# A gated cross-attention and mixture-of-experts block: queue orders of the attention written anew, scores of two pairs interleaved, one spread matmul a chunk

## The reference

```python
# attention of layernorm(x) to the context
q, k, v = proj(hs, Wq, bq), proj(at, Wk, bk), proj(at, Wv, bv)
scores = clip(einsum('bhsd,bhtd->bhst', q, k) / sqrt(32), -50, 50)
scores = clip(where(attend, scores, -10000.0), -50, 50)
probs = softmax(scores); probs = probs / (probs.sum(-1) + 1e-8)
delta = rs * ((probs @ v) @ Wo.T + bo)
x = x + tanh(g_xattn) * (layernorm(delta) * ln_gamma + ln_beta)
# experts on h = layernorm(x): 8 experts, the best 2 of each token
probs = softmax(h @ gate_weight.T); top_v, top_i = top_k(probs, 2)
y = sum_e w_e * (silu(gate_e) * up_e) @ down_e.T
x = x + tanh(g_ffn) * y
```

## Time and profile before

| | us |
|---|---|
| three runs | 991.68, 992.07, 988.66; median 991.68 |
| profiled execution | 987.01, of it span 984.8 |
| attention, to the last second layernorm | 0 to 264.6 |
| routing | 264.6 to 298.8 |
| expert loop | 298.8 to 984.8 |

### The profile page before, as it was taken

How to read it: one execution, slowest core, us unless ns; L and a number is a source line. 1 busy time by engine, 2 the same in 40 slices (tenths; PEclk the granted TensorE clock), 3 DMA queues, 4 the chain that set the end, 5 groups by cost and what they waited for, 6 DMA issues and landing times.

```text
span 984.8 us, 14350 instructions
## 1 busy us (share of the span) xinstructions
PE 910.5 (92%) x4217; PEld 714.1 (73%) x4218; DVE 450.3 (46%) x767; ACT 381.1 (39%) x717; POOL 257.3 (26%) x305
## 2 busy tenths in 40 slices
PE   4979999997819999999999999999999999999994
PEld 4746767664607888888888888888888888888883
DVE  5648778676586121261361352721452253217211
ACT  3555655643413222352452443522442253236221
POOL 4034627274231111122122122211131121122111
PEclk9999999997858999999999999999999999999997
DMA  7030121202636211171272262622352145121121
GB/s 305 13 117 0 71 102 48 79 37 93 240 114 269 43 21 32 33 276 33 42 267 37 60 245 43 240 61 40 105 204 32 21 134 186 21 42 22 21 43 21
DMA packets 27905, 93.92 MB, mean 95 GB/s; under 512 B 5424, under 2 KB 5424, under 8 KB 21104
## 3 DMA queue, kind: packets, MB, share of 16 engines
q1 hardware_dynamic: 18528, 72.03, 19.6%
q0 software_dynamic: 8640, 20.62, 11.0%
q10 hardware_dynamic: 720, 1.07, 0.3%
HBM read 75.03 MB, written 18.68 MB: 95 GB/s over the span
## 4 chain that ended last, share of the span: by engine, by line
PE 86%; DVE 4%; issue 3%; DMA 3%; ACT 2%; POOL 1%; SPq 0%; DVEq 0%; POOLq 0%; ACTq 0%
PE bank L255 76%; PE bank L1312 3%; DMA xs<-in_x 2%; PE bank L1299 2%; DVE rden L402 1%; PE bank L1138 1%; PE bank L1150 1%; PE bank L1184 1%; PE bank L1102 1%; PE bank L1171 1%; ACT hs L896 1%; DVE st_a L361 0%; DVE r_lo L406 0%; DMA xg<-h_rows,g_idx 0%; POOL tok_tile L822 0%
## 5 line engine op out<-in xcount | busy, mean ns | idle before, releaser
L255 PE MATMUL bank<-g_hi,gt_hi 128*128 128x512 f32 x592 | 237.5, 401 | 1.6 <-DVE gt_lo L662 1.6
L255 PE MATMUL bank<-g_hi,gt_lo 128*128 128x512 f32 x592 | 234.5, 396 | 0.0
L255 PE MATMUL bank<-g_lo,gt_hi 128*128 128x512 f32 x592 | 234.4, 396 | 0.0
L692 DVE TENSOR_TENSOR hid<-silu,bank 128x256 f32<-128x256 f32 x148 | 61.5, 420 | 309.0 <-ACT silu L1064 308.9
L1064 ACT ACTIVATE silu<-bank 128x256 f32<-128x256 f32 x148 | 56.6, 382 | 255.7 <-PE bank L255 253.5
L255 PEld LDWEIGHTS bank<-g_hi,gt_hi 128*128 128x128 f32 x592 | 111.6, 188 | 27.6 <-issue 2.0
L255 PEld LDWEIGHTS bank<-g_hi,gt_lo 128*128 128x128 f32 x592 | 111.4, 188 | 27.2
L255 PEld LDWEIGHTS bank<-g_lo,gt_hi 128*128 128x128 f32 x592 | 111.7, 189 | 25.8
L854 POOL COPY g_idx<-slot_idx 128x1 int32 x37 | 6.8, 183 | 471.3 <-ACT w_nxt L1078 471.3
L255 PE MATMUL bank<-dn_hi,hd_hi 128*128 128x512 f32 x296 | 126.4, 427 | 0.0
L255 PE MATMUL bank<-dn_lo,hd_hi 128*128 128x512 f32 x296 | 116.6, 394 | 0.0
(11 more groups left out here) (228 smaller groups left out, 1288.1 us busy)
## 6 DMA issues: line engine op xcount, KB each, us to landing
raw<-in_w_exp SPq DMA_DIRECT2D x48, 1024.0 KB, 5.3
raw<-in_w_attn SPq DMA_DIRECT2D x4, 1024.0 KB, 13.4
xs<-in_x SPq DMA_DIRECT2D x4, 1024.0 KB, 6.7
xr<-in_x SPq DMA_DIRECT2D x4, 1024.0 KB, 5.9
out_rows<-xr SPq DMA_DIRECT2D x16, 256.0 KB, 2.2
h_rows<-dh SPq DMA_DIRECT2D x16, 256.0 KB, 2.1
rows<-in_b_rows ACTq DMA_DIRECT2D x1, 1024.0 KB, 13.4
c_raw<-in_ctx_t SPq DMA_DIRECT2D x1, 640.0 KB, 3.8
```

The lines of the kernel that those rows point to most:

```text
L255: mm = eng.matmul(psum, a(k), b(k), start=(first and k == 0 and j == 0), stop=(last and k == n - 1 and j == 2))
L692: dve.tensor_tensor(hid[:, p, :], silu[:, p, :], bank[p][:, 256:512], ALU.mult).then_inc(hid_done, 1)
```

## The change

- PE: `scores(b, m)` computes two pairs at once, their six matmuls alternating between rows 0-63 and 64-127 and banks 4 and 5. `spread` makes one matmul a chunk: the high and the low part of the inverse lie at rows 0 and 32 of one tile `r_two`, the selection `bsel` in the same rows. `router` has the tokens stationary and the gate weights (8 columns) moving, so logits come out by token; `logits_by_token` is gone.
- `ex_hi` and `ex_lo` have four places (RING); `sc` and `ex` keep two. `normalise` writes in place into `o_un`, `o_n` is gone.
- `batch` is written anew on PE, ACT, DVE and POOL. Logits are kept by ACT in the batches, by DVE behind the last. `split_weight(3)` moves into batch 0. SP's wait for `w_lo_done` goes. POOL's setup has two more memsets and one more `affine_select`.

The diff, with the old bodies of `batch` and smaller edits left out (they stand above):

```diff
-        ex_hi = sb("ex_hi", [P, 2, S], F32R, pa)
-        ex_lo = sb("ex_lo", [P, 2, S], F32R, pa)
+        ex_hi = sb("ex_hi", [P, RING, S], F32R, pa)
+        ex_lo = sb("ex_lo", [P, RING, S], F32R, pa)
...
-        bsel = sb("bsel", [NH, KC, 4, HD], F32R, pa)
+        bsel = sb("bsel", [P, KC, 4, HD], F32R, pa)
...
-        rden = sb("rden", [NH, S], F32, pa)
-        r_hi = sb("r_hi", [NH, S], F32R, pa)
-        r_lo = sb("r_lo", [NH, S], F32R, pa)
+        rden = sb("rden", [LO_ROW + NH, S], F32, pa)
+        r_two = sb("r_two", [P, S], F32R, pa)
...
-        o_n = sb("o_n", [P, 2, S], F32, pa)
...
-            sp.wait_ge(w_lo_done, 4)
             def stores(n):
...
             def invert_sums(n):
...
-                dve.reciprocal(rden[:, :], den[:, :]).then_inc(den_r, 1)
+                dve.reciprocal(rden[0:NH, :], den[:, :]).then_inc(den_r, 1)
...
-                dve.tensor_scalar(r_hi[:, :], rden[:, :], 1.0, None, ALU.mult).then_inc(r_h, 1)
+                dve.tensor_scalar(r_two[0:NH, :], rden[0:NH, :], 1.0, None, ALU.mult).then_inc(r_h, 1)
...
-                dve.tensor_tensor(r_lo[:, :], rden[:, :], f32(r_hi[:, :]), ALU.subtract).then_inc(r_l, 1)
+                dve.tensor_tensor(r_two[LO_ROW:LO_ROW + NH, :], rden[0:NH, :], f32(r_two[0:NH, :]),
+                                  ALU.subtract).then_inc(r_l, 1)
             def normalise(n, m):
...
-                if m >= 2:
-                    dve.wait_ge(o_l, n * KC + m - 1)
-                dve.tensor_tensor(o_n[:, m % 2, :], bank[m % 2][:, :], o_un[:, m, :], ALU.mult).then_inc(o_nd, 1)
+                dve.tensor_tensor(o_un[:, m, :], bank[m % 2][:, :], o_un[:, m, :], ALU.mult).then_inc(o_nd, 1)
             def update_and_residual(n, u, r):
...
+            def keep_logits(n, t):
...
+                dve.tensor_copy(logits[:, bass.ds(n * TT + t, 1), :].rearrange("p a e -> p (a e)"),
+                                h_bank(t, True)[:, 0:E]).then_inc(lg_done, 1)
             def batch(b, back, front):
+                def clip(s):
+                    dve.wait_ge(s_mm, b * PAIRS + s + 1)
+                    if s >= 2 or back:
+                        dve.wait_ge(s_exp, b * PAIRS + s - 1)
+                    dve.tensor_scalar(sc[:, s % 2, :], bank[4 + s % 2][:, :], lim[:, bass.ds(b, 1)], -CLIP,
+                                      ALU.min, ALU.max).then_inc(s_clip, 1)
+                clip(0)
+                clip(1)
+                if back:
+                    normalise(b - 1, 0)
+                    normalise(b - 1, 1)
+                    v_low(b)
+                    normalise(b - 1, 2)
+                    normalise(b - 1, 3)
+                q_low(b, 2)
+                q_low(b, 3)
+                clip(2)
+                clip(3)
+                if front:
+                    ln_statistics(b + 1)
+                if back:
+                    update_and_residual(b - 1, 0, None)
+                clip(4)
+                clip(5)
+                if back:
+                    update_and_residual(b - 1, 1, 0)
+                    update_and_residual(b - 1, 2, 1)
+                else:
+                    split_weight(3)
+                if front:
+                    x_low(b + 1, 0)
+                    x_low(b + 1, 1)
+                clip(6)
+                clip(7)
+                if front:
+                    x_low(b + 1, 2)
+                    x_low(b + 1, 3)
+                if back:
+                    update_and_residual(b - 1, 3, 2)
...
                     k_low(b + 1)
...
+                    update_and_residual(b - 1, None, 3)
+                if front:
+                    q_low(b + 1, 0)
                 invert_sums(b)
+                if front:
+                    q_low(b + 1, 1)
...
-                dve.tensor_tensor(o_lo[:, m, :], o_n[:, m % 2, :], f32(o_hi[:, m, :]), ALU.subtract).then_inc(o_l, 1)
+                dve.tensor_tensor(o_lo[:, m, :], o_un[:, m, :], f32(o_hi[:, m, :]), ALU.subtract).then_inc(o_l, 1)
...
-                keep_logits(NB - 1, t, tail=True)
+                keep_logits(NB - 1, t)
             def split_lo(dst, hi, p, done):
...
+            for tile in (kbd_hi, kbd_lo, vbd_hi, vbd_lo, hsel, two_rows, bo_two, bsel, r_two):
...
+            pool.wait_ge(setup, 13)
...
+                pool.wait_ge(setup, 15 + i)
+                pool.affine_select(out=bsel[row:row + NH, :, :, :],
+                                   in_=rden[row:row + NH, :].rearrange("p (m a d) -> p m a d", m=KC, a=4),
+                                   compare_op=ALU.is_equal,
+                                   fill=0.0, base=0, pattern=[[-4, KC], [-1, 4], [0, HD]],
+                                   channel_multiplier=1).then_inc(setup, 1)
+            for i, row in enumerate((0, LO_ROW)):
+                pool.wait_ge(setup, 17 + i)
...
             def batch(b, back, front):
+                def ex_low(s):
+                    pool.wait_ge(e_h, b * PAIRS + s + 1)
+                    pool.tensor_tensor(ex_lo[:, s % RING, :], ex[:, s % 2, :], f32(ex_hi[:, s % RING, :]),
+                                       ALU.subtract).then_inc(e_l, 1)
+                ex_low(0)
+                ex_low(1)
+                if back:
+                    for m in range(KC):
+                        o_low(b - 1, m)
+                ex_low(2)
+                ex_low(3)
+                if back:
+                    add_beta(b - 1, 0)
+                if front:
+                    ln_inverse(b + 1)
+                if back:
+                    inverse_delta(b - 1, 0)
+                ex_low(4)
+                ex_low(5)
+                if back:
+                    inverse_delta(b - 1, 1)
+                    add_beta(b - 1, 1)
+                    inverse_h(b - 1, 0)
+                    add_beta(b - 1, 2)
+                    inverse_delta(b - 1, 2)
+                    inverse_h(b - 1, 1)
+                ex_low(6)
+                ex_low(7)
+                if back:
+                    add_beta(b - 1, 3)
+                    inverse_delta(b - 1, 3)
+                    inverse_h(b - 1, 2)
+                    inverse_h(b - 1, 3)
+            pool.wait_ge(setup, 19)
...
+            def keep_logits(n, t):
+                act.wait_ge(lg_mm, n * TT + t + 1)
+                act.activation(logits[:, bass.ds(n * TT + t, 1), :].rearrange("p a e -> p (a e)"),
+                               h_bank(t, False)[:, 0:E], ACT.Copy).then_inc(lg_done, 1)
             def batch(b, back, front):
+                def exp_and_high(s):
+                    act.wait_ge(s_clip, b * PAIRS + s + 1)
+                    if s >= 2 or back:
+                        act.wait_ge(e_l, b * PAIRS + s - 1)
+                    act.activation(ex[:, s % 2, :], sc[:, s % 2, :], ACT.Exp, scale=INV_SCALE).then_inc(s_exp, 1)
+                    act.wait_ge(s_exp, b * PAIRS + s + 1)
+                    if s >= RING or back:
+                        act.wait_ge(pair_mm, b * PAIRS + s - RING + 1)
+                    act.activation(ex_hi[:, s % RING, :], ex[:, s % 2, :], ACT.Copy).then_inc(e_h, 1)
+                def o_copy(m):
+                    act.wait_ge(pair_mm, b * PAIRS + 2 * m + 2)
+                    if back:
+                        act.wait_ge(o_l, (b - 1) * KC + m + 1)
+                    act.activation(o_un[:, m, :], bank[6][:, :], ACT.Copy).then_inc(o_ev, 1)
+                exp_and_high(0)
+                exp_and_high(1)
+                if back:
+                    o_high(b - 1, 0)
+                    o_high(b - 1, 1)
+                q_high(b, 2)
+                if back:
+                    o_high(b - 1, 2)
+                    o_high(b - 1, 3)
+                q_high(b, 3)
+                if back:
+                    o_copy(0)
+                exp_and_high(2)
+                exp_and_high(3)
+                if not back:
+                    o_copy(0)
+                exp_and_high(4)
+                exp_and_high(5)
+                o_copy(1)
+                if front:
+                    normalise_x(b + 1)
+                if back:
+                    normalise_h(b - 1, 0)
+                else:
+                    split_weight(3)
+                if front:
+                    x_high(b + 1, range(0, 2))
+                if back:
+                    normalise_h(b - 1, 1)
+                exp_and_high(6)
+                exp_and_high(7)
+                o_copy(2)
+                if front:
+                    x_high(b + 1, range(2, KC))
+                    act.wait_ge(s_mm, b * PAIRS + PAIRS)
+                    k_high(b + 1)
+                if back:
+                    h_copy(b - 1, 0)
+                    normalise_h(b - 1, 2)
+                if front:
+                    q_high(b + 1, 0)
+                if back:
+                    h_copy(b - 1, 1)
+                    keep_logits(b - 1, 0)
+                    normalise_h(b - 1, 3)
+                act.wait_ge(pair_mm, b * PAIRS + PAIRS)
```

(104 more changed lines are left out.)

176 lines of the change are left out of this document (13 added, 163 removed).

## The result

The changed kernel takes 984.6 us (median; 983.9 to 986.8), the kernel before on the same chips 989.1 (984.1 to 993.1): ratio 0.9952, 95% interval 0.9935 to 0.9969. That is 4.5 us, where 15.4 were forecast. The profiled execution of before (987.0, span 984.8) lies in the lower half of its range and that of after (986.4, span 984.6) at the upper end of its own, so the traces show less difference than the medians. The absolute time lies inside the forecast range; the gain is under a third of the forecast one.

The account below looks back on a forecast made before the run. Bound: TensorE's own queue in middle batches, busy 92% of the span. Batches -17.9, clock +3.2, slow DVE +3, tail -3.7 sum to -15.4 us; against 991.7 the forecast was 976.5 us, range 968 to 988.

Parts of the forecast that it names:

- the walk: Four engine queues followed through the attention batches: spread-to-spread 48.8, 49.2 and 42.1 us, first spread at 81.7.
- Rival (a): Scores: the couples do not overlap, 2.74 us of PE work come back in each batch; 982.5 us, chance 0.14.
- Router: Router with tokens stationary: eight passes take 0.6 us, at worst the old 0.97.
- PE's work: TensorE's work in a middle batch: 44 us by the sum of prices against 51, 43.3 in the queues followed.
- Waits: PE's new waits in a middle batch, among them for h copies and x_low: 5.8 us in sum.
- Rival (c): All queues: each engine waits 0.1 us longer at some 30 hand-overs, 3 us a batch; 988.5 us, chance 0.13.
- The clock, +3.2: Batch ends: TensorE's clock falls after idle and light work, 1.6 us counted twice more.
- Rival (b): Batch ends: the clock stays down, some 5 us in place of 1.6 at two or three ends; 984, chance 0.08.
- DVE beside POOL, +3: VectorE's packed queue: steps slowed beside POOL's work add 1 us for each of three batches.
- rival (d): VectorE becomes the bound as steps between SBUF tiles stretch threefold, +6 us a batch; 996 us, chance 0.08.
- Last batch: Last attention batch, spread to spread: 42.1 us against 47.57, a gain of 5.5.
- Tail, -3.7: Behind the last batch: o_product(0) ends 1.3 us earlier by fewer spreads, routing 2.4 earlier without logits transposes, with shorter routers.

Follow-up runs that it names:

- a_fill_all: The changed kernel, orders and waits kept, with unread matmuls in every idle or light stretch of PE in the attention: 975.6 us, ratio 0.9895 to the kernel before.
- b_apart: The kernel before with two pairs' scores in one block, three matmuls on rows 0-63, then three on 64-127, not in turn: 983.1 us, ratio 0.9933.
- a_fill: The changed kernel with 8 and 4 unread 512-column matmuls behind the transposes of h tiles 2 and 3, ends of batches 1 and 2: 981.1 us, ratio 0.9914.
- a_end_vlow: The changed kernel with h copies 2, 3 ahead of v_high, both transposes before their routers, and next batch's v_low moved to the batch before: 975.3 us, ratio 0.9872.
- a_tail: The changed kernel with h copies and transposes earlier at batch ends, unread matmuls there and ahead of the last h transposes and router: 974.9 us, ratio 0.9854.

## Why the prediction was wrong, point by point

From 0 to the experts' first matmul (298.8 us before) the walk, ahead of the two allowances, came to 277.2, the forecast with them to 283.4, the changed kernel to 298.9, and the changed kernel with filler to 288.4. Two things failed: the clock was allowed 3.2 us and took 10.5 (288.4 to 298.9), and with the clock held the walk was still 11.2 us short, for which the 3 us of slow DVE was the only allowance. Of the 15.5 us between forecast and changed kernel in these traces 7.3 are the clock's and 8.2 the walk's.

| | walk | after | a_fill_all |
|---|---|---|---|
| first spread | 81.7 | 84.9 | 81.3 |
| batch 1 | 48.8 | 53.9 | 52.4 |
| batch 2 | 49.2 | 54.9 | 52.1 |
| last batch | 42.1 | 47.2 | 45.7 |
| rest | 55.4 | 58.1 | 56.9 |

- **Couples:** right in price and mechanism, 0.89 us a block of two pairs. Rival (a) falls. The Trainium skill ("TensorEngine Tiling (Array Packing)", Key Properties) has different tiles run weight loads and matmuls in parallel, and the trace agrees; that the matmuls must alternate was my own addition, and `b_apart` refutes it.
- **Spreads:** right, two in 0.56 us (189.50 to the next `q_product` at 190.06 in a_fill). **Router:** 0.81 and not 0.6. I took the row of the transposes whose weights have 8 rows. The Trainium skill ("TensorE: Matmul & The Clock Gate", LDWEIGHTS) gives 107 ns for a load of 128 columns, 0.86 for eight as an estimate, and was nearer. It also says that the number of rows makes no difference; here a pass with 8 rows of weights took 0.07 us (twelve from 268.20 to 269.03 in the kernel before), one with 128 took 0.10 (0.81 for eight), and the measurement decides.
- **PE's work:** 48.4 us in a_fill_all's middle batches, less 12 fillers of 0.228, is 45.7; I had 43.3, so this term was 2.4 us too small in each. 0.8 is the router, 0.7 that I subtracted from a sum of prices, 50.8, where the row had 51.54, and 0.7 that the walk had 43.3 where the sum gave 44. It is under my bound of 46, and the waits are under that of 9: neither sign of being wrong showed the miss.
- **Waits:** 6.5 and 4.8 us a middle batch, 5.8 in the walk, at the places named a little less than walked (`h_copy(2)` 2.06, `h_copy(3)` 0.69, `x_low` 1.10 in batch 1, for 2.65, 0.8 and 1.45), and in batch 0 8.6 us (1.00, 1.22, 1.32, 2.73, 2.31) for 8.95. Not in the walk: 0.78 us a batch for `o_copy`, since `pv` of a chunk can't start while ACT copies the one before. Rival (c) falls: PE's waits are near those walked.
- **The clock, +3.2: the step that failed most.** I took the dip of before, 1.6 us, and counted it twice. But a dip costs by what runs in it: at a batch's end these were routers, transposes, scores, spreads and part of a `q_product`. In batch 2 the busy time is 50.07 against 45.7 of work, 4.4 us of clock. By the table the clock costs 1.5 and 2.8 us of the middle stretches (the filler itself takes time there), 1.5 of the last and 1.2 of the tail; ahead of these stand 1.9 us in batch 0 (from the first score to the first spread: 41.64 us, 39.76 in a_fill_all) and 1.7 for the dip at 26 us. I had walked the waits of batch 0, the last batch and the tail and had asked of none of them what they did to the clock. Rival (b) names this cause, at two or three ends and with 0.08; it was at every light place. Its 984 is near the measured time by luck in part, since it kept the walk's work.
- **DVE beside POOL, +3:** `v_low` took 5.13 us and 3.8 was counted, and in batch 1 `pv(0)` starts 1.60 us late, 0.10 behind its end, for 0.15 in the walk:

```profile
87.99 5.14 DVE L394 TENSOR_TENSOR vbd_lo<-v_all,vbd_hi 64x128 fp32r<-64x128 f32 x4
...
93.23 0.47 PE L253 MATMUL bank<-ex_hi,vbd_hi 128*128 128x512 f32 x1 [1.60 <-issue]
```

  In `a_end_vlow` this wait is gone, and the two middle stretches together are 1.3 us shorter. `xr`, also from SBUF to SBUF, did not stretch (0.81 us in the mean of batch 2, 1.04 before), so rival (d) falls. The rest of the allowance hides part of the miss.
- **Last batch:** 47.2 for 42.1. It begins at half clock, and ACT copies the sums at 233.50, 3.0 us after my time for it (38.4 behind the first score at 192.08), behind `normalise_h(3)`, which waits for POOL. `r_two` is ready at 238.61, but the spread is held by the routers at half clock and the copy of their logits, until 240.88. With the clock held 1.5 of the 5.1 goes. Of the 3.6 that stay some 0.9 is the filler's own, since in a_fill_all `r_two` is ready at 230.57 and the spread starts at 231.50 behind five fillers; the rest is the sums' copy, still 2.2 us late there, and the inverse.
- **Tail, -3.7:** -1.1 measured. The transposes of the logits are gone, but a router took 1.71 us where before's last two took 1.04, and the time from the last matmul of the `o_product`s to the first matmul of the ranks is 17.6 against 17.1 before. `a_tail` shows the forecast's shape: 15.3. After:

```profile
262.57 1.72 PE L1242 MATMUL bank<-gate_w,ht 128*128 128x8 f32 x8
264.13 1.09 PE L1236 MATMUL bank<-ident,dh 128*128 128x128 f32 x4
265.02 1.71 PE L1242 MATMUL bank<-gate_w,ht 128*128 128x8 f32 x8
266.59 1.09 PE L1236 MATMUL bank<-ident,dh 128*128 128x128 f32 x4
267.47 3.42 PE L1242 MATMUL bank<-gate_w,ht 128*128 128x8 f32 x16
```

and `a_tail`:

```profile
253.82 0.60 PE L1239 MATMUL bank<-ident,dh 128*128 128x128 f32 x4
254.26 0.96 PE L1245 MATMUL bank<-gate_w,ht 128*128 128x8 f32 x8
...
257.64 0.95 PE L1245 MATMUL bank<-gate_w,ht 128*128 128x8 f32 x8
```

- **The baseline:** I forecast against 991.7, the median of three runs (less 15.4 that is 976.3; I wrote 976.5); with more runs the kernel before is at 987 to 990.5. This flatters the forecast: the absolute time is 8.1 us off, the gain 10.9.

Still open: what lets the dip at 26 us come and go, in the old order and in the new. In the seven traces in which the x transposes there are slow (1.53 to 1.97 us) PE had waited 3.00 to 3.38 us ahead of them; in the eight in which they take 1.09 it had waited 2.65 us or less, in the two with filler there 0 and 1.26. The wait always ends near 26 us, so the dip goes with how early PE was done before it; why that differs is not shown.

## What to carry to other kernels

An order that takes work out of a busy TensorE and puts waits among short instructions paid twice here: price each such place at half clock for all that runs until it is back, not as a fixed fee. Test it cheaply with matmuls that nobody reads; where they help, mend the order (here 984.6 to 967.9 by moving some lines on ScalarE, VectorE and TensorE), and the filler is then hardly needed. Measure the content in the old order before writing a new one: here the content alone gave about twice the gain of the whole change.
